# Two heads' value products in one slot of the score loop, and signals cleared by ranges

## The reference, cut to what matters

```
q = latents @ Wq
kv = concatenate([x, latents], axis=1) @ Wkv      # x: the context, 64 rows; latents: 512 rows
k, v = split(kv, 2)                               # heads of width 64: 16 (layers 1, 2) or 8 (layer 3)
q, k = l2norm(q) * q_scale, l2norm(k) * k_scale   # layers 2 and 3, in forms of their own
attn = softmax(mask(q @ k.T * SCALE))             # 512 queries x 576 keys for each head and batch
out = (attn @ v) @ Wo                             # layer 3: then a layer norm
```

## Time and profile before

| | |
|---|---|
| three runs | 4181.42, 4185.76 (median), 4192.54 us |
| the profiled execution, its own time | 4151.07 us |
| its span, from the first to the last instruction | 4149.3 us |
| mean granted clock of TensorE, share of full speed | 0.909 |
| PE / PEld busy | 3610.8 us (87%) / 2138.9 us (52%) |
| DVE, ACT, POOL busy | 2194.2, 1391.1, 1387.4 us |

### The profile page before, as it was taken

One profiled execution on the slowest core, in us unless ns is written; L12 is line 12 of the kernel. 1 busy time (PEld: TensorE's weight loads), 2 busy tenths in 40 slices (PEclk: granted clock), 3 DMA queues, 4 the chain that ended last, 5 costly groups with the idle time before them and its releaser, 6 DMA issues. The chain is left out here.

```text
span 4149.3 us, 51536 instructions
## 1 busy us (share of the span) xinstructions
PE 3610.8 (87%) x17482; PEld 2138.9 (52%) x17482; DVE 2194.2 (53%) x5071; ACT 1391.1 (34%) x2991; POOL 1387.4 (33%) x1992
## 2 busy tenths in 40 slices
PE   7898879899999876888798999997995879995996
PEld 5675665455545573333344455555672434444663
DVE  5374354564644684555356566665233356665443
ACT  3243104343433561222144444442231134441221
POOL 2142332332423362322253544542213144443011
PEclk9999879999999886888699999998898789997998
DMA  2001000000000000000000000002221000005121
GB/s 95 1 1 59 14 30 15 1 1 1 1 1 1 12 1 22 1 1 1 34 13 1 1 1 1 1 1 84 91 81 39 0 27 1 1 1 209 54 69 61
DMA packets 49123, 106.62 MB, mean 26 GB/s; under 512 B 6564, under 2 KB 38692, under 8 KB 46692
## 3 DMA queue, kind: packets, MB, share of 16 engines
q1 hardware_dynamic: 42724, 86.53, 5.8%
q0 software_dynamic: 6144, 16.79, 1.3%
HBM read 74.72 MB, written 28.57 MB: 25 GB/s over the span
## 5 line engine op out<-in xcount | busy, mean ns | idle before, releaser
L2578 POOL TENSOR_SCALAR probs<-probs,inv_sum 128x512 f32<-128x512 f32 x640 | 435.0, 693 | 966.7 <-DVE inv_sum L2699 966.4
L2536 ACT ACTIVATE probs<-psum_banks,neg_max 128x576 f32<-128x576 f32 x640 | 468.5, 737 | 712.9 <-DVE neg_max L2778 711.1
L2778 DVE TENSOR_REDUCE neg_max<-psum_banks 128x1 f32<-128x576 f32 x640 | 455.1, 753 | 192.8 <-PE psum_banks L2411 186.2
L2411 PE MATMUL psum_banks<-keys_T,queries_T 64*128 64x288 f32 x2560 | 408.4, 439 | 40.0 <-ACT probs L2536 27.8
L2708 DVE COPY probs_T<-psum_banks 128x512 f32<-128x512 f32 x640 | 409.4, 681 | 20.0 <-PE psum_banks L2340 20.0
L2411 PEld LDWEIGHTS psum_banks<-keys_T,queries_T 64*128 64x128 f32 x2560 | 226.0, 190 | 268.6 <-ACT probs L2536 161.1
L2340 PE MATMUL psum_banks<-ident,probs 128*128 128x128 f32 x2560 | 353.1, 281 | 3.2 <-POOL probs L2578 2.3
L2340 PEld LDWEIGHTS psum_banks<-ident,probs 128*128 128x128 f32 x2560 | 277.5, 142 | 130.7 <-POOL probs L2578 73.4
L2370 PE MATMUL psum_banks<-probs_T,values 128*64 128x512 f32 x1280 | 307.3, 604 | 2.2 <-issue 2.2
L4279 PE MATMUL psum_banks<-w_L_experts_up,sorted_T 128*128 x552 | 255.7, 600 | 0.4 <-issue 0.3
L4215 POOL DMA_INDIRECT normed<-expert_outputs,row_index x64 | 65.6, 1025 | 416.2 <-DMA expert_outputs<-expert_rows 397.9
(11 more groups left out here) (523 smaller groups left out, 6336.6 us busy)
## 6 DMA issues: line engine op xcount, KB each, us to landing
expert_outputs<-expert_rows SPq DMA_DIRECT2D x92, 128.0 KB, 1.7
group_normed_T<-sorted_rows SPq DMA_DIRECT2D x20, 512.0 KB, 4.1
w_L_experts_down<-in_L_experts_down SPq DMA_DIRECT2D x2, 4096.0 KB, 34.1
row_vectors<-in_rows SPq DMA_DIRECT2D x1, 5120.0 KB, 35.3
sorted_rows<-zero_rows SPq DMA_DIRECT2D x4, 1024.0 KB, 9.2
w_L_xattn_Wkv<-in_L_xattn_Wkv SPq DMA_DIRECT2D x2, 2048.0 KB, 8.8
w_L_experts_up<-in_L_experts_up SPq DMA_DIRECT2D x1, 4096.0 KB, 12.5
x_res<-in_x SPq DMA_DIRECT2D x4, 512.0 KB, 7.0
```

Of the source, the lines that this page charges most:

```text
L2411: last = pe.matmul(k.ps[:, 2 * h + a, 0:HALF], qT[r, b % 2, j, t * P:(t + 1) * P], kT[r, j, k0:k0 + HALF], start=True, stop=True)
L2536: act.activation(prob[:, g % PB, h * w:(h + 1) * w].rearrange("p (a n) -> p a n", a=2), k.ps[:, 2 * h:2 * h + 2, 0:HALF], ACT.Exp, bias=nm ...
L2578: pool.tensor_scalar(w, w, inv[:, g % 4, h:h + 1], 1.0, ALU.mult, ALU.mult).then_inc(shared, 1)
L2778: dve.tensor_reduce(nmax[:, g % 4, h:h + 1], k.ps[:, 2 * h:2 * h + 2, 0:HALF], AX.XY, ALU.max, negate=True).then_inc(maxed, 1)
```

## The change

In `attended` the two halves become one: all 20 instructions of a pair come in slot 4j + 6, and none in slot 4j + 7. The context values get a buffer twice as large, filled with zeros once by POOL: head 0's values lie in partitions 0 to 63 of one half of it and head 1's in partitions 64 to 127 of the other, and the context product of a head takes all 128 rows of `context_probs_T`, of which 64 meet zeros. So it has the form of a fifth block of 128 keys. The units are laid into other slots, so that none lies in a slot 4j + 6 except one turn of layer 3. The mask's own buffer goes (the mask is changed in place). `signals` clears runs of neighbouring semaphores by one instruction each, in all stages.

```diff
-        for s in sems:
-            nc.gpsimd.sem_clear(s)
+        nums = sorted(s.num for s in sems)
+        for n in nums:
+            if n - 1 not in nums:
+                last = n
+                while last + 1 in nums:
+                    last += 1
+                nc.gpsimd.sem_clear(range(n, last + 1))
         nc.all_engine_barrier()
...
     if a == 2:
-        values = [0, 1, 2, 3, 4, 5, 8, 9, 12, 13]
-        outs = [16, 17, 20, 21, 24, 25, 28, 29]
-        turns = [26, 27]
+        values = [0, 1, 3, 4, 5, 7, 8, 9, 11, 12]
+        outs = [15, 16, 17, 19, 20, 21, 23, 24]
+        turns = [27, 28]
         stats, spread, shift = 16, 21, 10
     else:
-        values = [0, 1, 2, 3, 4]
-        outs = [5, 8, 9, 12]
+        values = [0, 1, 3, 4, 5]
+        outs = [7, 8, 9, 11]
         turns = [14, 15]
...
-        vc = k.sb("context_values", [P, PAIRS, NC], st)
+        vc = k.sb("context_values", [P, 2, PAIRS, NC], st)
...
-                def attended(b, j, part):
+                def attended(b, j):
...
-                    for c in ((0, 1), (2, 3, 4))[part]:
+                    for c in range(TT + 1):
                         for h in range(2):
                             r = slice(64 * h, 64 * h + 64)
                             if c < TT:
                                 last = pe.matmul(k.ps[r, 6, :], v[:, c, (2 * j + h) * 64:(2 * j + h + 1) * 64],
                                                  pT[:, q % 2, h, c, :], start=c == 0, stop=False)
                             else:
-                                last = pe.matmul(k.ps[r, 6, :], vc[r, j, :], pTc[r, q % 2, :], start=False, stop=True)
-                    if part == 1:
-                        last.then_inc(valued, 1)
+                                last = pe.matmul(k.ps[r, 6, :], vc[:, h, j, :], pTc[:, q % 2, :], start=False,
+                                                 stop=True)
+                    last.then_inc(valued, 1)
...
-                        if s >= 4 + LAG and (s - 4 - LAG) % 4 < 2:
-                            attended(b, (s - 4 - LAG) // 4, (s - 4 - LAG) % 4)
+                        if s >= 4 + LAG and (s - 4 - LAG) % 4 == 0:
+                            attended(b, (s - 4 - LAG) // 4)
...
+                        act.wait_ge(zeroed, 1)
                         for h, sem in ((0, ctx_value_moved), (1, value_moved)):
                             r = slice(64 * h, 64 * h + 64)
-                            act.copy(vc[r, 4 * a:4 * a + 4, :], k.ps[r, 7, :].rearrange(
+                            act.copy(vc[r, h, 4 * a:4 * a + 4, :], k.ps[r, 7, :].rearrange(
                                 "p (j s d) -> p j s d", s=2, d=64)[:, :, h, :]).then_inc(sem, 1)
...
                 batch_rstd(0)
+                pool.memset(vc[:, :, :, :], 0.0).then_inc(zeroed, 1)
```

More of the change, by code:

```diff
@@ L2154, in latent_attention @@
         crs = k.sb("context_rstd", [P, 2, B], st)
-        km = k.sb("key_mask", [P, B * NC], st) if mask else None
+        km = kmask[:, 0, :] if mask else None
         if unit:
@@ L2209, in latent_attention @@
                 "ctx_copied", "valued", "stored", "value_made", "value_moved", "out_made", "out_added", "biased",
-                "ctx_value_moved", "small_loaded", "kv_loaded", "q_loaded", "o_loaded", "y_stat", "y_aggr", "y_shift", "y_rstd", "y_scaled") as (
+                "ctx_value_moved", "zeroed", "small_loaded", "kv_loaded", "q_loaded", "o_loaded", "y_stat", "y_aggr", "y_shift", "y_rstd", "y_scaled") as (
                 scored, masked, maxed, exped, sum_inverted, shared, prob_turned, copied, ctx_copied, valued, stored,
-                value_made, value_moved, out_made, out_added, biased, ctx_value_moved, small_loaded,
+                value_made, value_moved, out_made, out_added, biased, ctx_value_moved, zeroed, small_loaded,
                 kv_loaded, q_loaded, o_loaded, y_stat, y_aggr, y_shift, y_rstd, y_scaled), nc.Block() as block:
@@ L2354, in turn_context_probs @@
                     last.then_inc(prob_turned, 1)
-                def attended(b, j, part):
+                def attended(b, j):
                     q = b * PAIRS + j
[L2359 to L2365, removed]
-                    for c in ((0, 1), (2, 3, 4))[part]:
+                    pe.wait_ge(copied, 8 * q + 8)
+                    pe.wait_ge(ctx_copied, q + 1)
+                    if q >= 1:
+                        pe.wait_ge(stored, q)
+                    pe.wait_ge(value_moved, b * NV + (TT + 1) * (j // 4 + 1))
+                    pe.wait_ge(ctx_value_moved, b * A + j // 4 + 1)
+                    for c in range(TT + 1):
                         for h in range(2):
@@ L2443, in _ @@
                             step(i, i0, i1)
-                    attended(b, PAIRS - 1, 0)
-                    attended(b, PAIRS - 1, 1)
+                    attended(b, PAIRS - 1)
                     if b + 1 < B:
@@ L2757, in _ @@
                 if mask:
-                    dve.tensor_scalar(km[:, :], kmask[:, 0, :], 1.0, -1.0, ALU.min, ALU.add).then_inc(mask_made, 1)
+                    dve.tensor_scalar(km, km, 1.0, -1.0, ALU.min, ALU.add).then_inc(mask_made, 1)
                     dve.wait_ge(mask_made, 1)
-                    dve.tensor_scalar(km[:, :], km[:, :], 1e30, None, ALU.mult).then_inc(mask_made, 1)
+                    dve.tensor_scalar(km, km, 1e30, None, ALU.mult).then_inc(mask_made, 1)
                     dve.wait_ge(mask_made, 2)
```

## The result

The changed kernel takes 4255.14 us (median of 4 runs, 4241.06 to 4261.69) against 4186.12 us before (4181.42 to 4192.54, 4 runs): 1.0159 times as long, with a 95% interval of 1.013 to 1.0188; the medians differ by 69 us. The forecast was 57 more, 4243 us, in a range of 4214 to 4276.

The account below looks back on a forecast made before the run. Each slot was taken to cost the larger of PE's work and the dependency loop. Slots 102, ends of batches -20.5, clears -32 and clock +7 gave +57 us on the runs' median: 4243 us, range 4214 to 4276.

Parts of the forecast that it names:

- What bounds the slots: Layers 1 to 3: a slot costs the larger of PE's work and the dependency loop, 3.69 or 4.03 us.
- The merge: Product slots: twenty products in a row cost 4.45 us instead of 4.74, 0.29 saved per pair; merged slot 6.65.
- The slots: Slots of layers 1, 2 and 3 lose 35, 44 and 22 us, together 102.
- The ends of batches: Last slot to next projections: these wait for exponentials, about 3.8 us instead of 6.00 in layer 1; 20.5 saved in all.
- Layer 3's statistics: Layer norm's statistics on DVE come one slot earlier, with less cover: up to 0.4 us lost three times.
- Waits: First products don't wait for the moved context values, 0.7 us to spare; ACT's wait for the zeros costs nothing.
- Clearing: Closings of stages: 483 single semaphore clears become about 30, at 0.070 us each, 32 us saved.
- rival (a): Closings: range clears priced by count, 0.044 us each, so 12 instead of 32 us saved, 4263 us; chance 8%.
- The clock: Thin slots of layers 2 and 3: PE's clock falls 4 times more, 7 us lost.
- Rival (b): Clock falls behind every second thin slot, some 25 more times at 2 us: 4286 us or more; chance 8%.
- The sum: Whole kernel: 102 - 20.5 - 32 + 7 = +57 us, 4243 us, 1.4% slower.
- Rival (d): Loop behind a long slot gets shorter, 0.6 us less in 80 slots, making it even, 4190 us; chance 4%.

Follow-up runs that it names:

- the run with both edits: Changed kernel with two matmuls nobody reads in thin slots and layer 3's output statistics and norm one slot later: 4214.28 us, ratio 1.0138 to the kernel before.
- the filler: Changed kernel with two matmuls nobody reads in slot 2 and in context-turn slots without value or out: 4237.94 us, ratio 1.0114 to the kernel before.
- the run with the old lists: Changed kernel with the units in their old slots and semaphores cleared one by one: 4267.02 us, ratio 1.0269 to the kernel before.

## Why the prediction held, point by point

**What bounds the slots.** Right, and to the hundredth: 6.64 for 6.65, 3.69, 3.91, 4.02, 4.36. "A slot costs the larger of both" is shown by the run without mask.

**The merge.** Forecast at 0.29 us less work per pair. The context's form gives 0.14 of it by itself, and the pair's slots went from 4.06 + 4.92 to 6.64 with one start of 2.20 less, so joining the halves gives the other 0.14 or 0.15. What a single change of form costs is not shown: the context's form took out one such change, and joining took out two.

**The slots.** 102 us forecast. At full clock layer 1 lost 8.7, 8.5, 8.5 and 9.4 us, 35.2 in all for 35 forecast. Layers 2 and 3 lost 45.4 and 30.7 us between first and last slots, 76.1 for 66; the difference is the clock (7.9), the longer slot 13 (2.5), and the uneven slot 0.

**The ends of batches.** Mis-sized: 20.5 forecast. In layer 1 the stretch from slot 31 to the next batch's first slot fell from 40.56 to 38.93, 1.6 us for the 2.35 forecast (2.2 and the merge's 0.15). The step that failed is "they wait for the exponentials instead". Between slot 31 and the projections stand eight more transposes, which wait 1.19 us for DVE's copies, and DVE makes these behind the maxima: the projections start 4.52 us into the end, where I had 3.8. In layer 2 it was 0.9 to 1.5, in layer 3 1.6 and 2.4. The 2.4 is behind batches 1 and 2, where the norm, moved with the outs, no longer lies in the last slot: there PE waits 0.79 us for DVE's unit rows instead of 1.45. All nine ends between batches gave 14.7 us for 16.8 forecast, even without their share of the last pairs' merge. The three behind a last batch gave 1.8, 1.5 and 0.9, 4.2 us for 2.7. So 18.9 of 20.5 were measured; two errors partly made each other good.

**Layer 3's statistics.** Named, at up to 0.4 us three times; slot 13 was 1.0, 0.9 and 0.6 us over its 4.35, in batch 1 with the clock falling near its end. This timeline of the changed kernel, batch 2, shows why:

```profile
3721.38 1.24 PE L2415 MATMUL psum_banks<-keys_T,queries_T 64*128 64x288 f32 x8 [1.76 <-ACT probs L2540]
...
3721.84 1.39 DVE L2730 BATCH_NORM_STATS2 out_stat<-projected 128x6 f32<-128x256 f32 x4
...
3723.93 1.42 DVE L2783 TENSOR_REDUCE neg_max<-psum_banks 128x1 f32<-128x576 f32 x2
...
3726.09 0.63 PE L2357 MATMUL psum_banks<-ident,context_probs 128*128 128x128 f32 x4 [2.44 <-DVE probs_T L2713]
```

The maxima begin 2.55 us into the slot, behind the statistics; in the run with both edits they began at 1.62. Two of the falls came over slot 14 right behind. That PE's idle time led to them fits, since with the filler slot 13 was as long and they did not come.

**Waits.** Right for the products: in the slots none waited. "ACT's wait for the zeros costs nothing" holds too, but the zeros cost something in another place. POOL writes them while DVE normalises the batch's first rows, and the first of DVE's four instructions beside it took 0.97 us instead of 0.41, in layers 1 and 2 of every kernel that has the zeros. In layer 1 PE waits for it. Kernel before, then changed kernel:

```profile
621.39 1.38 DVE L2652 TENSOR_SCALAR batch_normed<-x_res,batch_mv,batch_rstd 128x256 f32<-128x256 f32 x4
622.83 1.11 PE L2267 MATMUL psum_banks<-ident,batch_normed 128*128 128x128 f32 x4 [0.35 <-DVE batch_normed L2652]
...
613.64 0.99 POOL L2618 MEMSET context_values<- 128x1024 f32 x1
613.81 1.94 DVE L2657 TENSOR_SCALAR batch_normed<-x_res,batch_mv,batch_rstd 128x256 f32<-128x256 f32 x4
615.80 1.11 PE L2272 MATMUL psum_banks<-ident,batch_normed 128*128 128x128 f32 x4 [0.90 <-DVE batch_normed L2657]
```

That is 0.55 us, once. In layers 2 and 3 PE's next wait is shorter by as much, and nothing is lost.

**Clearing.** 32 forecast, 30.2 by the profile. There are 42 clears instead of 30, since a list's numbers lie in several runs, and a clear of many does take longer, up to 264 ns against 44: the single ones that stand for 21, 29 and 42 clears took 151, 194 and 264 ns, 5.4 for each further semaphore where rival (a) had 44. So rival (a) had the mechanism but not its size: all 42 last 4.1 us together.

**The clock.** 7 us for 4 falls more; it was 7 falls more and 7.9 us (12.8 against 4.9). That the us came out is luck: nearly twice the falls forecast, at 1.3 us each instead of the 1.75 taken. Rival (b) would have asked for some 25.

**The sum.** The terms in the three stages were +88.5 by forecast (102 - 20.5 + 7), and 94.5 were measured: 111.3 in the slots (2.3 over the forecast with its clock, mostly slot 13), 18.9 back at the ends (1.6 short), and 2.1 in front of the first slots, where nothing was forecast (layer 1's clock and the zeros, less layer 2's gain). The closings gave back 30.2 for 32. That makes 64.3. The stages that the change leaves alone, without the two that differ by chip, took 3.0 more in this profile, where clock stretches lie differently: 67.3 in all, and the medians, of other executions too, differ by 69. So the 57 was short by 6 in the three stages, by 2 at the closings, and by 3 that are none of the change's. Rival (d), a shorter loop behind a long slot, did not occur: slots 7, 11, ... without a unit took the full 3.69 in the run with the old lists. Its sum was off besides: 80 x 0.6 makes 48 of the 57 us good, which gives 4195 us and not 4190.

## What to carry to other kernels

In a pipeline of slots a slot costs the larger of its engine's work and its dependency loop. Before work is gathered to save its fixed costs, add up what the slots it leaves will cost: here 0.29 us of work was saved per pair, and the merge took over 1 us back, since the emptied slot kept its loop of 3.69 or 4.02. Of a change with several parts each should be priced and tried alone; two parts of this one (the clears, the context's form) were gains, and kept by themselves they beat both kernels.

## What the runs showed of the hardware

- A context product of 128 rows, half of them zeros, costs less than one of 64 rows, in this place, between products of 128 rows and the scores: 0.96 us for four instead of 1.00, and it starts 0.10 us earlier behind the products.
- The same instructions took 22 to 28 us longer in layer 2's feed-forward stage on chip 4 than on chips 1 and 11. Absolute times of different chips can't be set against each other at this size.
- A clear of semaphores by a range lasted 44 ns for one, 151 for 21, 194 for 29 and 264 for 42; one by one they stood 70 ns apart.
- A DVE instruction of 128x256 took 0.97 us beside a memset of 128x1024 on POOL, and 0.41 without it; that they hinder each other is seen in all ten kernels with the memset and in neither of the two without.
- PE's clock fell 10 times in each of three profiles whose slots of 4.02 us left PE idle for 1.76 us, and 3 and 5 times with two idle matmuls laid into most of them. In layer 1's slots of 3.69, with 1.42 us idle, it never fell.
